# Destination one-hots of a sorted group, made by one comparison of two tensors

## The reference, cut to what matters

```
h = relu(layernorm(x)); x = x + segment_sum((h * node_vec1)[src], dst) * node_vec1_n2   # layer one
h = relu(layernorm(x)); x = x + (1 + eps) * h + segment_sum(relu(h[src] + edge_attr), dst)  # layer two
```

## Time and profile before

| | us |
|---|---|
| median of 3 runs (4801.01 to 4810.65) | 4802.91 |
| the profiled execution | 4791.23 |
| its span in the trace | 4789.2 |
| TensorE busy (matmuls) | 3721.2 |
| VectorE busy | 3812.7 |
| ScalarE busy | 3261.3 |
| GpSimd busy | 3497.5 |

### The profile page before, as it was taken

The page is one execution under the profiler, slowest core; times in us unless marked ns, Lnnn a source line. Parts: engine busy times, 40 slices in busy tenths (PEclk is TensorE's granted clock), DMA queues, the critical chain, the costliest instruction groups (busy, mean ns, idle before and its releaser), DMA issues.

```text
span 4789.2 us, 130194 instructions
## 1 busy us (share of the span) xinstructions
PE 3721.2 (78%) x43852; PEld 2888.9 (60%) x43852; DVE 3812.7 (80%) x11454; ACT 3261.3 (68%) x9090; POOL 3497.5 (73%) x3590
## 2 busy tenths in 40 slices
PE   0388888888888888888888899467767777777775
PEld 0266666666666666666666666356666666666664
DVE  9788888888888888888888886767777776777775
ACT  1377777777777777777777777456666766666664
POOL 6757777777777777777777777477777777777774
PEclk9999999999999999999999999778888888888887
DMA  6322222222222222222222221211212221211221
GB/s 111 63 51 54 57 54 54 54 56 54 54 54 56 54 53 54 56 54 53 54 56 54 53 54 44 72 39 54 57 43 54 57 57 54 58 49 48 57 57 26
DMA packets 439702, 262.77 MB, mean 55 GB/s; under 512 B 334660, under 2 KB 423732, under 8 KB 432632
## 3 DMA queue, kind: packets, MB, share of 16 engines
q1 hardware_dynamic: 322488, 187.55, 16.7%
q0 software_dynamic: 110816, 60.69, 6.7%
q10 hardware_dynamic: 5728, 5.82, 0.5%
HBM read 172.96 MB, written 80.85 MB: 53 GB/s over the span
## 4 chain that ended last, share of the span: by engine, by line
PE 32%; POOL 23%; DVE 19%; issue 13%; ACT 10%; DMA 2%; DVEq 1%; ACTq 0%; SPq 0%; POOLq 0%
POOL stage L759 22%; PE candidates L1247 18%; PE plain_ps L1259 7%; DVE arena L1753 7%; ACT message L987 5%; DVE arena L1729 4%; ACT centered L956 2%; PE sorted_agg L1187 2%; PE candidates L1157 1%; ACT arena L880 1%; POOL message L759 1%; PE key_rows L1230 1%; DMA stage<-in_edge_attr 1%; DVE counts L1475 1%; PE key_rows L1139 1%
## 5 line engine op out<-in xcount | busy, mean ns | idle before, releaser
L771 POOL DMA_INDIRECT records<-stage,place_i x1875 | 1879.0, 1002 | 696.2 <-issue 652.0
L759 POOL DMA_INDIRECT stage<-table,src_plain x1250 | 1246.9, 997 | 409.1 <-issue 377.3
L987 ACT ACTIVATE message<-candidates,member_is 128x96 bf16<-128x96 f32 x4560 | 1170.7, 377 | 429.4 <-PE candidates L1247 426.3
L1753 DVE TENSOR_SCALAR arena<-window_iota,dst_rel 128x224 bf16<-128x224 f16 (+1 forms) x4800 | 1091.2, 302 | 37.8
L880 ACT ACTIVATE arena<-key_rows 125x640 f16<-125x640 f16 x1000 | 653.2, 716 | 215.1 <-DVE arena L1729 83.2
L1187 PE MATMUL sorted_agg<-arena 128*96 128x224 bf16 (+1 forms) x5000 | 654.1, 285 | 161.0 <-DVE arena L1753 109.6
L1259 PE MATMUL plain_ps<-summed,message 128*96 128x224 bf16 x4560 | 609.2, 269 | 68.2 <-ACT message L987 68.2
L1187 PEld LDWEIGHTS sorted_agg<-arena 128*96 128x96 bf16 x5000 | 543.7, 137 | 186.1 <-issue 118.6
L1259 PEld LDWEIGHTS plain_ps<-summed,message 128*96 128x96 bf16 x4560 | 490.7, 128 | 269.6 <-ACT message L987 127.4
L1729 DVE TENSOR_SCALAR arena<-arena,row_key 125x1280 bf16<-125x1280 f16 x1000 | 554.7, 555 | 96.5 <-ACT arena L880 64.6
L1139 PE MATMUL key_rows<-ident,record 128*125 128x128 f16 x5000 | 425.8, 235 | 239.2 <-DMA record<-records 96.2
(11 more groups left out here) (228 smaller groups left out, 5139.0 us busy)
## 6 DMA issues: line engine op xcount, KB each, us to landing
record<-records SPq DMA_DIRECT2D x50, 1650.0 KB
stage<-in_edge_attr SPq DMA_DIRECT2D x125, 400.0 KB, 3.2
records<-pad SPq DMA_DIRECT2D x25, 1650.0 KB, 11.9
records<-stage,place_i POOLq DMA_INDIRECT x1875
stage<-table,src_plain POOLq DMA_INDIRECT x1250
message<-table,mid_src POOLq DMA_INDIRECT x288
xs<-in_x SPq DMA_DIRECT2D x8, 390.6 KB
table<-parts ACTq DMA_DIRECT2D x4, 585.9 KB
```

Source lines behind the costliest of these rows:

```text
L759: pool.indirect_dma_start(message[:, k, j, :] if l == 0 else rows[:, k, j, :], None, table0 if l == 0 else table1, bass.IndirectOffsetOnAx ...
L771: pool.indirect_dma_start(records, bass.IndirectOffsetOnAxis(ap=place_i[:, h, e:e + 1], axis=0), stage[:, h, e, :], None).then_inc(scatter ...
L987: last = nc.scalar.activation(direct_message[n % DB][:, m * WIDE:(m + 1) * WIDE], candidates[n % 2][:, m * WIDE:(m + 1) * WIDE], ACT.Copy, ...
L1753: last = nc.vector.tensor_scalar(dst_onehot(g, t), window_iota[:, 0:WA if tile == 0 else WT], dst_rel[:, h, tile:tile + 1], None, ALU.is_e ...
```

## The change

In layer one, VectorE's part of a group's destination one-hots becomes a single tensor_tensor: its first operand is the iota row, repeated for each tile (tile axis with step zero), its second the group's relative destinations, read as fp16 from the record, each repeated along the 224 columns (inner axis with step zero). `some` are the tiles that it makes: 1 to 9 in group 0, 0 to 9 in group 1, 0 to 8 in groups 2 to 9. The wide first tile of a batch stays a tensor_scalar. So that the tiles lie at even distances, a tile 0 that is 224 wide now lies at the end of the 320 columns reserved for it (from `UP = WA - WT` on) and not at their start. The pauses within a group (`dst_paused`) are gone in layer one. Layer two keeps its loop over tiles.

```diff
-            room = dst_room[:, g % 2, 0:WA] if t == 0 else dst_room[:, g % 2, WA + (t - 1) * WT:WA + t * WT]
-            return room if g == 0 and t == 0 else room[:, 0:WT]
+            if g == 0 and t == 0:
+                return dst_room[:, 0, 0:WA]
+            return dst_room[:, g % 2, UP + t * WT:UP + (t + 1) * WT]
+
+        def dst_onehots_of(g, some):
+            return dst_room[:, g % 2, UP + some.start * WT:UP + some.stop * WT].rearrange("p (t w) -> p t w", w=WT)
...
                     if l == 0:
-                        paused = (6 + 2 * (GROUPS - 2)) * b + (3 * g if g < 2 else 6 + 2 * (g - 2))
+                        some = range(1 if g == 0 else 0, tiles)
+                        if g == 0:
+                            nc.vector.tensor_scalar(dst_onehot(0, 0), window_iota[:], dst_rel[:, h, 0:1], None, ALU.is_equal)
+                        shape = [P, len(some), WT]
+                        ends = record16[:, 0, g * GROUP + some.start:g * GROUP + some.stop, 2 * F + 1]
+                        nc.vector.tensor_tensor(dst_onehots_of(g, some), window_iota[:, 0:WT].unsqueeze(1).to_broadcast(shape),
+                                                ends.unsqueeze(2).to_broadcast(shape), ALU.is_equal).then_inc(dst_onehot_ready[0], 1)
+                        return
                     for t in range(tiles):
```

## The result

The kernel after the change takes 4956.7 us (median of 4 runs, 4955.3 to 4963.4) against 4802.0 before (4 runs beside it, 4800.1 to 4810.7): ratio 1.0321, interval 1.0303 to 1.0339. It is 155 us slower; the forecast was 147 us slower, 4950. The profiled execution's span grew by 165.2 us, from 4789.2 to 4954.4.

What follows compares the result with a forecast made beforehand. GpSimd, with only 76 us to spare over 22 batches, was taken as deciding: 24 x 9.4 = 226 us of held issues, less 79 us slack, adds 147 to 4803, giving 4950 us. Range 4835 to 5105 us.

Steps and rivals of the forecast that it cites:

- S: Extra time GpSimd's issues lose per layer-one batch, held by long comparisons: 11.2 less today's 1.8, 9.4 us.
- each group lets one issue pass at its start: Sorted stage: from group 3, one GpSimd issue passes, the next meets the comparison 1.22 us in and waits 0.91 us.
- The slack: GpSimd's spare time, 76 us over 22 batches, plus 3 us at the record's landing, absorbs part of the loss.
- (a): Sign: the new comparison takes some 2.25 us for 2016 elements; 1.2 us would mean two elements a step.
- (b): Sign: VectorE's period in the sorted stage stays near 3.4 us.
- (c): Sign: fewer than 26 scatters in the sorted stage, one in two near 1.9 us; 75 take 107 us, not 98.
- (d): Sign: GpSimd's idle times before a scatter set are gone in nearly all batches.
- (f): Sign: the last batch's 38 gathers begin near 3148 us, not 3010; layer two's length is unchanged.
- (e): Sign: TensorE waits some 7 us a batch for the records before turning the next batch's keys.
- it decides from S = 3.3 us on: Condition for GpSimd's lateness to slow the kernel: S above 3.3 us a batch, 79 / 24.
- Two elements a step: Rival: comparisons take 1.22 us, ScalarE's 2.81 us a group bounds the stage, kernel faster at 4775 us; chance 0.07.
- No difference: Rival: VectorE's time is equal, GpSimd's issues fall in gaps or lateness is absorbed, 4803 +- 10 us; chance 0.08.

Runs made afterwards that it cites:

- experiment 1: Changed kernel with the iota operand read from PSUM, ranking scans in steps of 16 instead of 20: 4811.2 us, ratio 1.0031 against the kernel before.
- experiment 2: Changed kernel with each group's comparison cut into three pieces, signal after the last: 4844.3 us, ratio 1.0099 against the kernel before.
- experiment 6: Kernel before with eight more mid gathers a batch into unused columns, VectorE untouched: 4952.2 us, ratio 1.0327.
- experiment 3: Changed kernel with the iota row also as second operand, unit step on both, output changed: 4784.9 us, ratio 0.9971 against the kernel before.
- experiment 4: Changed kernel with 1 instead of 12 mid gathers a batch from layer one's second batch on: 4938.0 us, ratio 1.0270 against the kernel before.
- experiment 7: Changed kernel with few gathers, and SyncE's edge loads and padding held past TensorE's loop return: 4891.9 us, ratio 1.0184 against the kernel before.
- experiment 9: Kernel before with only SyncE's edge loads and padding held past TensorE's loop return: 4790.9 us, ratio 0.9971.

## Why the prediction was right

**The size of S, the term that decided.** Forecast 9.4 us a batch. Over the 22 batches the scatters grew by 1864.2 - 1643.8 = 220.4 us, 10.0 a batch, and the gathers, which met other instructions, shrank by 17.7, 0.8 a batch: 9.2 net. That this is so near to 9.4 is in part luck. Counted over 0.95 us an issue in 22 batches, the scatters that start between a batch's first and last destination one-hot lose 10.4 us each batch, before 1.4; forecast were 11.2 and 1.8. So the stage gave 9.0. Scatters outside it lost another 1.0, which no term of the prediction had, and the gathers gave back 0.8. In the stage shown, the first issues of groups 0, 1 and 2 lost 1.1, 1.2 and 1.0 us, where the prediction had 1.5, 1.2 and 1.5. Of the steps behind it, "each group lets one issue pass at its start; the next comes 1.22 us into it" and waits 0.91 us, holds within 0.02 us: 1568.20 - 1566.96 = 1.24 us into it, 1.85 us long, 0.90 over 0.95. The phase read at one short-instruction run carried over: an issue held to a comparison's end is followed by one that starts just ahead of the next. Experiments 1 and 2 show that the hold is the cause, and experiment 6 that GpSimd time of that size is enough.

**The slack.** 220.4 - 17.7 = 202.7 us less the spare used, 76.1 - 7.7 = 68.4, is 134.3, the growth of the 22 batches. This only adds up GpSimd's list, and would hold for any cause; the forecast in it is that the spare is used up before TensorE pays. That GpSimd at a busy share of 75% (of these batches) had 3.5 us a batch left was the number to have for the kernel after; experiment 3 shows the same floor from the other side.

**VectorE.** 2.25 us forecast, 2.26 to 2.28 in the sorted stage; period 3.3 to 3.4 us forecast, 3.42 measured. A change of nothing there, and experiment 1, with GpSimd out of it, is within 14 us of before.

**The signs.** (a), (b) as above. (c) 21 scatters in the stage, not 26, mean 1436 ns; sets of 75 last 106 to 109 us, against 96 to 98 before. (d) GpSimd's idle before a set is gone but for 1.6 us in a few batches. (f) The last batch's 38 gathers:

```profile
3161.67 1.09 POOL L763 DMA_INDIRECT message<-table,src_plain  x1 [4.67 <-PE plain_ps L1263]
```

3161.7 against the 3148 forecast: 151.7 us after where it was, not 138. 134 of it is the 22 batches; 12 had come before them, where the first two sets took 217.0 us in place of 206.9; the rest is behind them. These gathers themselves and what lies up to layer two took 9.0 more (forecast 9.4).

**Where a step was off.** (e) "TensorE will then stand still about 7 us a batch" holds in 14 batches (102.9 us, 7.3 each), but not in every batch. In the nine between them TensorE reaches the keys late by itself and waits 1.3 us or less: its pause at the loop's return, in each of these, costs 6.0 us in place of 3.2 (53.9 in all, from 28.7). The prediction had no such term. It did not move the total here, since GpSimd sets the period with or without it (experiment 6, 56.8 us of such pauses, same time). Nor had it the ring of start, set, load and landing. Both together cost nearly as much as the full list does, as experiments 4 and 7 show; the condition "it decides from S = 3.3 us on" tells only of the list. And layer two was not unchanged: it took 4.5 us more (165.2 - 160.7), for which I have no cause. The terms sum to 134 + 12 + 5 + 9 + 4.5 = 165 of the profiled span; the runs' medians differ by 155, since the profiled execution of before lies 11 us under the median of its four runs.

**Rivals.** Two elements a step fell at (a), and experiment 3 gives its price, 4785 us against the 4775 I had. No difference fell at (c).

## What to carry to other kernels

Before several short VectorE instructions are joined into one with two SBUF operands, look at who issues indirect DMAs on GpSimd: here each issue that started inside the long one waited for its end. Reckon GpSimd's spare as span less busy less the gap behind every issue, not from its busy share. And where a wait on the path is removed, reckon the whole ring of one iteration (start condition, issues, load, landing) before counting the freed time as gained; an operand in PSUM, or shorter pieces, took most of the hold away here, though neither version was quicker than the kernel before.

## What the hardware showed that I had not expected

- A VectorE comparison of 2.26 us holds no GpSimd issue up when one of its inputs is in PSUM: 1004 ns a scatter against 1130, at the same VectorE time.
- TensorE's pause at a loop's return is not a constant: 3.2 us on average before (28.7 / 9), 6.0 after (53.9 / 9), 6.4 in experiment 4, and 1.2 to 1.4 with the edge loads held back (experiments 9 and 7). It ends 2.6 to 3.4 us after a 16 KB packet of an instruction queue starts.
- A moving operand with a step of ten bf16 elements: 579 ns a product of 224 columns against 270 with a unit step, and 416 against 120 ns of TensorE's busy time each, at a granted clock of 0.85 against 0.95.
